# GpSimd adds the chunks for the layer norm of a projection stage, and three engines' orders change

## The chip, the cores and the metric

The kernel runs on one core of one Trainium2 chip. The metric is the device time of one execution in microseconds. Engines are named PE (TensorE), DVE (VectorE), ACT (ScalarE), POOL (GpSimd) and SP (SyncE, which here only issues DMAs).

## The reference, cut to what matters

The input `x` is (4, 1024, 256) in float32. Four blocks follow one another: latent attention, a feed-forward block, a selective scan and a second feed-forward block, each with a layer norm ahead and a residual. Only the first part of the attention is touched:

```
m = mean(x, -1); v = var(x, -1); xn = (x - m) / sqrt(v + 1e-5)
ct_q  = xn @ Wd_q_w + Wd_q_b            # 256 -> 128
query = (ct_q @ Wu_q_w + Wu_q_b) + rope(ct_q @ Wq_r_w + Wq_r_b)
ct_kv = xn @ Wd_kv_w + Wd_kv_b          # 256 -> 128
key   = (ct_kv @ Wu_k_w + Wu_k_b) + rope(xn @ Wk_r_w + Wk_r_b)
value = ct_kv @ Wu_v_w + Wu_v_b
```

## The kernel before, in words

The first stage is the function `project`. It goes over 4096 tokens in NT = 8 tiles of TW = 512 tokens. A tile is kept with its 256 features on partitions, in DC = 2 chunks `c` of 128. The stages after it (`attend`, then merging of heads, feed-forward, scan, feed-forward) are blocks of their own that begin when `project` is over.

Each engine runs a list of its own in program order, and semaphores hold an instruction until what it needs is there. An engine never passes over a waiting instruction. What a tile does:

- PE: `turn(t)` (L298) transposes tile t of x into `tr_bank`. `mean(t)` (L312) multiplies x by a matrix of 1/256, a product for each chunk, into `norm_bank`. `var(t)` (L323) does the same with the squares. `latent(t, 1)` and `latent(t, 0)` (L330) are the latent products for keys/values and for queries; `rotary` (L340), `compact` (L357) and `values` (L367) are the products behind them. A product of 128x512 in float32 takes two matmul instructions.
- ACT: `keep_x` (L427) copies the transposed tile to `xT`; `square` (L432); `guess` (L440), a first inverse root by Ln and Exp; `keep_latent` (L450); `high` (L456) and `middle` (L463) round `full` and then `rest` to bfloat16.
- DVE: `centre` (L494) subtracts the mean; `finish` (L504) does the root's Newton step in three instructions; `rotate` (L519), `join` (L533) and `keep_v` (L553) make keys, queries and values from the products.
- POOL: `scale(t)` (L266) multiplies the centred chunks by the inverse root, which gives `xn`, the input of `latent(t, 1)`. `lower_parts(t, side)` (L253) subtracts the rounded parts: first both chunks of `rest` (waiting for `high`), then both of the last part (waiting for `middle`). Side 1 is keys, side 0 queries.
- SP: the loads of x, and the stores of the three bfloat16 parts to `qk_parts`, 16 DMAs for a tile. In tile 3 it also loads the first groups' stacks.

The order on PE in a tile t is: `latent(t,1)`, `rotary(t,1)`, `latent(t,0)`, `values(t)`, `compact(t,1)`, `var(t+1)`, `rotary(t,0)`, `turn(t+2)`, `compact(t,0)`, `mean(t+2)`. ACT does `high(t-1,0)`, `keep_latent(t,1)`, `keep_latent(t,0)`, `square(t+1)`, `middle(t-1,0)`, `guess(t+1)`, `keep_x(t+2)`, `high(t,1)`, `middle(t,1)`. DVE does `rotate(t,1)`, `centre(t+1)`, `keep_v(t)`, `join(t,1)`, `finish(t+1)`, `rotate(t,0)`, `join(t,0)`. POOL does `lower_parts(t-1,0)`, `scale(t+1)`, `lower_parts(t,1)`. After the last tile PE and DVE compute row maxima for the first attention group (L413, L579).

Of the kernel before, what the change touches and what calls it, by code (L numbers as in the profile page):

```python
# [9 lines left out]
ALU = mybir.AluOpType  # L10
# [3 lines left out]
P = 128  # L14
B, S, D = 4, 1024, 256
T = B * S
TW = 512
NT = T // TW
TPB = S // TW
DC = D // P  # L20
# [108 lines left out]
def project(nc, io, xT, vT, split_scr, begun):  # L129
# [7 lines left out]
    with ExitStack() as ctx:  # L137
        m = Mem(nc, ctx)
        ident, row_max, neg_max, neg_rest, neg_parts = (
            begun[n] for n in ("ident", "row_max", "neg_max", "neg_rest", "neg_parts"))  # L140
        mean_w = m.sb("mean_w", [P, P])
# [12 lines left out]
        xc = m.sb("xc", [P, DC, TW])  # L154
        sq = m.sb("sq", [P, DC, TW])
        log_var, guess_rs, rs = (m.sb(n, [P, TW]) for n in ("log_var_p", "guess_rs_p", "rs_p"))
        xn = m.sb("xn", [P, 2, DC, TW])
        ct = m.sb("ct", [P, 2, TW])
        rot = m.sb("rot", [P, SIDES, 4, TW])
# [14 lines left out]
        proj_ready, latent_kept, rotated = m.sem("proj_ready"), m.sem("latent_kept"), m.sem("rotated")  # L174
        summed, high_kept, mid_kept = m.sem("summed"), m.sem("high_kept"), m.sem("mid_kept")
        rest_ready, low_kept, v_kept = m.sem("rest_ready"), m.sem("low_kept"), m.sem("v_kept")
        stack_in, neg_in = m.sem("first_stack_in"), m.sem("first_neg_in")
        unit_ready, unit_max, top_ready, turned, neg_ready, neg_split, ones_set = (
            m.sem(n) for n in ("unit_ready", "unit_max", "top_ready", "first_turned", "first_neg", "first_split", "first_ones"))
# [13 lines left out]
        UNITS = 12  # L193
# [6 lines left out]
        def parts_of(side):  # L200

            return (1 - side) * DC
# [41 lines left out]
        @block.gpsimd  # L244
        def _(pool):
            nc.gpsimd.memset(mean_w[:], 1.0 / D).then_inc(consts_set, 1)
            nc.gpsimd.memset(eps_col[:], EPS).then_inc(consts_set, 1)
            pool.wait_ge(consts_set, 2)
            for g in range(2):
                nc.gpsimd.memset(begun[f"ks{g}"][SROWS:MROWS], 1.0).then_inc(ones_set, 1)  # L250
                pool.wait_ge(ones_set, g + 1)

            def lower_parts(t, side):  # L253
                for u in (parts_of(side), parts_of(side) + 1):
                    k = t * CHUNKS + u
                    pool.wait_ge(high_kept, k + 1)
                    if t:

                        pool.wait_ge(low_kept, k - CHUNKS + 1)
                    nc.gpsimd.tensor_tensor(rest[:, u], full[:, u], parts[:, u, 0], ALU.subtract).then_inc(rest_ready, 1)  # L260
                for u in (parts_of(side), parts_of(side) + 1):

                    pool.wait_ge(mid_kept, t * CHUNKS + u + 1)
                    nc.gpsimd.tensor_tensor(parts[:, u, 2], rest[:, u], parts[:, u, 1], ALU.subtract).then_inc(low_kept, 1)

            def scale(t):  # L266

                pool.wait_ge(rs_step, t * 3 + 3)
                if t > 1:

                    pool.wait_ge(proj_ready, (t - 2) * UNITS + Q + 1)
                for c in range(DC):
                    nc.gpsimd.tensor_tensor(xn[:, t % 2, c], xc[:, c], rs[:], ALU.mult).then_inc(normed, 1)

            scale(0)
            for t in range(NT):
                if t:
                    lower_parts(t - 1, 0)
                if t + 1 < NT:
                    scale(t + 1)  # L280
                lower_parts(t, 1)
            lower_parts(NT - 1, 0)
            pool.wait_ge(neg_ready, 1)
            nc.gpsimd.tensor_copy(neg_parts[:, 0, 0], neg_max[:, 0]).then_inc(neg_split, 1)
            pool.wait_ge(neg_split, 1)
            nc.gpsimd.tensor_tensor(neg_rest[:, 0], neg_max[:, 0], neg_parts[:, 0, 0], ALU.subtract).then_inc(neg_split, 1)
            pool.wait_ge(neg_split, 2)
            nc.gpsimd.tensor_copy(neg_parts[:, 0, 1], neg_rest[:, 0]).then_inc(neg_split, 1)
            pool.wait_ge(neg_split, 3)
            nc.gpsimd.tensor_tensor(neg_parts[:, 0, 2], neg_rest[:, 0], neg_parts[:, 0, 1], ALU.subtract)\  # L290
                .then_inc(neg_split, 1)

        @block.tensor
        def _(pe):
# [17 lines left out]
            def mean(t):  # L312

                pe.wait_ge(x_kept, t * DC + DC)
                if t:

                    pe.wait_ge(rs_step, (t - 1) * 3 + 1)
                for c in range(DC):
                    mm = nc.tensor.matmul(norm_bank[:], mean_w[:], xT[:, c, t * TW:(t + 1) * TW],
                                          start=(c == 0), stop=(c == DC - 1))  # L320
                mm.then_inc(mean_ready, 1)

            def var(t):  # L323

                pe.wait_ge(squared, t * DC + DC)
                for c in range(DC):
                    mm = nc.tensor.matmul(norm_bank[:], mean_w[:], sq[:, c], start=(c == 0), stop=(c == DC - 1))
                mm.then_inc(var_ready, 1)

            def latent(t, u):  # L330

                if u == 0:
                    pe.wait_ge(latent_kept, t * 2 + 1)
                elif t:
                    pe.wait_ge(latent_kept, t * 2)
                for k in range(DC):
                    mm = nc.tensor.matmul(lat_bank[:], (wdq, wdkv)[u][:, k], xn[:, t % 2, k], start=(k == 0), stop=(k == DC - 1))
                mm.then_inc(proj_ready, 1)

            def rotary(t, side):  # L340
                for c in range(DC):
                    cols = slice(c * P, (c + 1) * P)
                    if side == 1:
                        if t:

                            pe.wait_ge(rotated, (t - 1) * SIDES * ROTS + ROTS + 2 * c + 2)
                        for k in range(DC):
                            mm = nc.tensor.matmul(rot_bank[c], wkr[:, k, cols], xn[:, t % 2, k],
                                                  start=(k == 0), stop=(k == DC - 1))
                    else:  # L350

                        pe.wait_ge(latent_kept, t * 2 + 2)
                        pe.wait_ge(rotated, t * SIDES * ROTS + 2 * c + 2)
                        mm = nc.tensor.matmul(rot_bank[c], wq[:, 1, cols], ct[:, 0], start=True, stop=True)
                    mm.then_inc(proj_ready, 1)
# [26 lines left out]
            mean(0)  # L382
            turn(1)
            var(0)
            mean(1)
            pe.wait_ge(consts_in, CONSTS)
            for t in range(NT):
                pe.wait_ge(normed, t * DC + DC)
                latent(t, 1)
                rotary(t, 1)  # L390
                latent(t, 0)
                values(t)
                compact(t, 1)
                if t + 1 < NT:
                    var(t + 1)
                rotary(t, 0)
                if t + 2 < NT:
                    turn(t + 2)
                compact(t, 0)
                if t + 2 < NT:  # L400
                    mean(t + 2)

            pe.wait_ge(stack_in, 2 * STACK_LOAD)
            for n in range(PAIRS):
# [18 lines left out]
        def _(act):  # L423
# [49 lines left out]
            for t in range(NT):  # L473
                if t:
                    high(t - 1, 0)
                keep_latent(t, 1)
                keep_latent(t, 0)
                if t + 1 < NT:
                    square(t + 1)
                if t:  # L480
                    middle(t - 1, 0)
                if t + 1 < NT:
                    guess(t + 1)
                if t + 2 < NT:
                    keep_x(t + 2)
                high(t, 1)
                middle(t, 1)
# [4 lines left out]
        def _(dve):  # L492
# [23 lines left out]
                nc.vector.scalar_tensor_tensor(rs[:], rs[:], 1.5, guess_rs[:], ALU.add, ALU.mult)\  # L516
                    .then_inc(rs_step, 1)

            def rotate(t, side):  # L519
                half = t % TPB  # L520
                bias = bcol[:, 2 + 4 * side:4 + 4 * side]
                cos, sin = (table[:, half * TW:(half + 1) * TW] for table in (cosT, sinT))
                r = rot[:, 1 - side]
                if t:

                    dve.wait_ge(summed, (t - 1) * CHUNKS + parts_of(side) + DC)
                for c, tables in enumerate(((cos, sin), (sin, cos))):
                    dve.wait_ge(proj_ready, t * UNITS + (ROT_K if side == 1 else ROT_Q) + c + 1)
                    for i, table in enumerate(tables):
                        nc.vector.scalar_tensor_tensor(r[:, 2 * c + i], rot_bank[c], bias[:, c:c + 1], table,  # L530
                                                       ALU.add, ALU.mult).then_inc(rotated, 1)

            def join(t, side):  # L533
                n = t * SIDES * ROTS + (1 - side) * ROTS
# [29 lines left out]
            finish(0)  # L564
            dve.wait_ge(consts_in, CONSTS)
            for t in range(NT):
                rotate(t, 1)
                if t + 1 < NT:
                    centre(t + 1)
                keep_v(t)  # L570
                join(t, 1)
                if t + 1 < NT:
                    finish(t + 1)
                rotate(t, 0)
                join(t, 0)
            for n in range(PAIRS):
                half, i = n // (PAIRS // 2), n % (PAIRS // 2)
# [1636 lines left out]
```

## Time and profile before

| | us |
|---|---|
| median of 3 runs (2103.42 to 2106.32) | 2104.65 |
| the profiled execution | 2105.05 |
| its span, first to last instruction | 2103.3 |
| PE busy | 1938.0 (92%) |
| DVE busy | 1676.9 (80%) |
| ACT busy | 1062.5 (51%) |
| POOL busy | 755.2 (36%) |
| mean granted TensorE clock | 0.955 of full speed |

Busy shares are over the whole program. `project` is its first 206 us, so these shares say little of the stage that changes; it has to be read tile by tile.

### The profile page before, as it was taken

The page shows a single profiled execution, that of the slowest core. Times are in us where ns is not written, and L with a number is a line of the kernel's source. Part 1 is how long each engine was busy: PE and PEld are TensorE (multiplying, and loading weights), DVE is VectorE, ACT ScalarE, POOL GpSimd, SP SyncE. Part 2 cuts the span into 40 slices and gives each one's busy share as a digit, 9 for nine tenths or more (in the row PEclk, how much of TensorE's full clock was granted, in tenths as well). Part 3 has the DMA queues.
Part 4 walks back from the last instruction along what each step waited for, and adds up shares of the span by engine and source line. Part 5 has one row for each costly group of instructions (what it writes and reads, how often), then busy time and mean ns, then how long its engine had stood idle before and what let it go on. Part 6 is the DMA issues. An engine that isn't in the chain of part 4 may idle for free. (4 is left out here: it accounts for less than half of the span.)

```text
span 2103.3 us, 25351 instructions
## 1 busy us (share of the span) xinstructions
PE 1938.0 (92%) x6834; PEld 728.0 (35%) x6834; DVE 1676.9 (80%) x2442; ACT 1062.5 (51%) x1399; POOL 755.2 (36%) x517
## 2 busy tenths in 40 slices
PE   8997999999999999999999997788888988799997
PEld 4441332322232323322444443233333333244443
DVE  5889998998998988964565578999999999945554
ACT  3541666665666666672222236576557557422221
POOL 4662110000000000000100029999999999810000
PEclk9996999999999999999999998999999989999998
DMA  3652112321211121213100013444444445300000
GB/s 103 142 128 52 41 42 45 66 45 42 42 47 42 41 47 41 41 50 118 40 0 0 0 62 92 125 114 118 117 115 116 117 117 152 88 0 20 20 10 31
DMA packets 94539, 138.23 MB, mean 66 GB/s; under 512 B 13600, under 2 KB 52656, under 8 KB 92880
## 3 DMA queue, kind: packets, MB, share of 16 engines
q1 hardware_dynamic: 94416, 136.73, 26.1%
q8 instruction: 61, 1.00, 0.2%
q14 instruction: 62, 0.51, 0.1%
HBM read 110.21 MB, written 26.08 MB: 65 GB/s over the span
## 5 line engine op out<-in xcount | busy, mean ns | idle before, releaser
L915 DVE TENSOR_REDUCE mx<-max_bank 128x1 f32<-128x512 f32 x960 | 617.9, 686 | 64.6 <-PE max_bank L824 64.3
L901 ACT ACTIVATE probs<-score_bank 128x1024 f32<-128x1024 f32 x512 | 496.9, 1021 | 289.2 <-PE score_bank L838 289.0
L824 PE MATMUL max_bank<-ks,qs 96*128 96x512 bf16 x960 | 335.6, 390 | 0.0
L838 PE MATMUL score_bank<-qs,ks 99*128 99x512 bf16 x1024 | 313.2, 389 | 14.9 <-issue 10.2
L1700 POOL TENSOR_TENSOR ring<-u,bc 128x1024 f32<-128x1024 f32 x128 | 302.6, 2374 | 0.0
L1770 PE MATMUL ys_bank<-outs,rec_diag 128*128 128x512 f32 x512 | 253.9, 626 | 45.6 <-POOL outs L1708 23.0
L884 PE MATMUL o_bank<-probs,vg 128*32 128x512 f32 x2048 | 275.4, 610 | 0.7 <-ACT probs L901 0.7
L1708 POOL TENSOR_TENSOR outs<-ring,bc 128x1024 f32<-128x1024 f32 x109 | 258.7, 2373 | 26.3 <-DVE ring L2079 26.3
L784 POOL CAST neg_parts<-neg_max 16x128 bf16<-16x128 f32 x31 | 8.8, 282 | 656.9 <-DVE neg_max L928 656.9
L1935 ACT ACTIVATE a_bank<-dt,decay_s 128x512 f32<-128x512 f32 x256 | 169.4, 684 | 147.4 <-DVE ring L2079 105.6
L1451 ACT ACTIVATE relu_f<-hid_bank_f 128x512 f32<-128x512 f32 x128 | 76.5, 597 | 327.3 <-PE hid_bank_f L1376 282.3
L1501 DVE SCALAR_TENSOR_TENSOR hid_f<-hid_bank_f,relu_f 128x512 f32<-128x512 f32 x128 | 86.8, 687 | 187.1 <-ACT relu_f L1451 186.1
L1352 PE MATMUL y_bank_f<-hid_f,wpr_f 128*128 128x512 f32 x512 | 234.2, 592 | 0.5 <-DVE hid_f L1501 0.5
L2070 DVE SCALAR_TENSOR_TENSOR ring<-a_bank,ring 128x512 f32<-128x512 f32 x256 | 171.4, 670 | 27.1 <-ACT a_bank L1935 26.8
L824 PEld LDWEIGHTS max_bank<-ks,qs 96*128 96x128 bf16 x960 | 94.1, 98 | 281.0 <-DVE mx L915 186.7
L1770 PEld LDWEIGHTS ys_bank<-outs,rec_diag 128*128 128x128 f32 x512 | 100.5, 200 | 186.7 <-issue 132.7
L1022 POOL TENSOR_TENSOR sq_sum_f<-sq_f 128x512 f32<-128x512 f32 x16 | 20.3, 1267 | 391.4 <-ACT sq_f L1049 391.4
L838 PEld LDWEIGHTS score_bank<-qs,ks 99*128 99x128 bf16 x1024 | 99.7, 100 | 122.9 <-issue 27.3
L1352 PEld LDWEIGHTS y_bank_f<-hid_f,wpr_f 128*128 128x128 f32 x512 | 95.9, 190 | 120.7 <-issue 115.8
L2079 DVE TENSOR_TENSOR_SCAN ring<-a_bank,ring 128x512 f32<-128x512 f32 x112 | 135.6, 1210 | 0.0
L2079 DVE TENSOR_TENSOR_SCAN ring<-a_bank,state,ring 128x512 f32<-128x512 f32 x106 | 134.7, 1271 | 0.0
L1376 PE MATMUL hid_bank_f<-xn_f,wfc_f 128*128 (+1 forms) x256 | 119.5, 600 | 3.2 <-POOL eps_col_f L991 3.2
(216 smaller groups left out, 2149.4 us busy)
## 6 DMA issues: line engine op xcount, KB each, us to landing
bc<-bc_scr SPq DMA_DIRECT2D x128, 512.0 KB, 4.9
qk_parts<-parts SPq DMA_DIRECT2D x128, 96.0 KB, 1.9
qs<-qk_parts SPq DMA_DIRECT2D x128, 64.0 KB, 4.1
o_scr<-o_sb SPq DMA_DIRECT2D x32, 256.0 KB, 2.1
ks<-qk_parts SPq DMA_DIRECT2D x16, 384.0 KB, 4.7
xin<-in_x_dram SPq DMA_DIRECT2D x8, 512.0 KB, 3.9
ks<-qk_parts SPq DMA_DIRECT2D x16, 256.0 KB, 3.5
qs<-qk_parts SPq DMA_DIRECT2D x32, 128.0 KB, 4.7
```

What stands on the lines that cost most here:

```text
L824: nc.tensor.matmul(max_bank[(r + a) % MB][:], qs[r][0:SROWS, half, j, qt * P:(qt + 1) * P], ks[r][0:SROWS, j, kh * TW:(kh + 1) * TW], star ...
L838: mm = nc.tensor.matmul(score_bank[pair][:, j % 2], ks[r][0:MROWS, j, kt * P:(kt + 1) * P], qs[r][0:MROWS, qh, j, :], start=True, stop=True)
L884: mm = nc.tensor.matmul(o_bank[32 * j:32 * j + 32, :], vg[r][:, kt, j], probs[:, s % 2, j], start=(kt == 0), stop=(kt == QT - 1))
L901: nc.scalar.activation(probs[:, s % 2, 2 * pair:2 * pair + 2], score_bank[pair][:], ACT.Exp, scale=SOFTMAX_SCALE).then_inc(probs_ready, 1)
L915: nc.vector.tensor_reduce(mx[:, a // HU, a % HU:a % HU + 1], max_bank[(r + a) % MB][:], AX_X, ALU.max)\
L1352: mm = nc.tensor.matmul(y_bank[c][:], wpr[:, f, c * P:(c + 1) * P], hid[:, f], start=(f == 0), stop=(f == FC - 1))
L1700: nc.gpsimd.tensor_tensor(ring[:, g % RING], u[t % 2][:], bc[:, g % BC, 0:1].to_broadcast([P, DC, TW]), ALU.mult).then_inc(inputs, 1)
L1708: nc.gpsimd.tensor_tensor(outs[:, g % OUTS], ring[:, g % RING], bc[:, g % BC, 1:2].to_broadcast([P, DC, TW]), ALU.mult).then_inc(weighted, 1)
L1770: mm = nc.tensor.matmul(y_bank[f][:], rec_diag[:, f * NS + n], outs[:, g % OUTS, f], start=(n == 0), stop=(n == NS - 1))
L1935: nc.scalar.activation(a_bank[g % 2][:, f], dt[:, t % 2, f], ACT.Exp, scale=a_col[:, f, n:n + 1])\
L2070: nc.vector.scalar_tensor_tensor(x, a, 1.0, x, ALU.subtract, ALU.mult).then_inc(scaled, 1)
L2079: nc.vector.tensor_tensor_scan(a if on_dve(g) else x, a, x, state[:, f, n:n + 1] if t % TPB else 0.0, ALU.mult, ALU.add)\
```

## The change

POOL adds the two chunks of x and the two chunks of the squares into new buffers `x_sum` and `sq_sum`, and for every tile but the first `mean` and `var` are then one product each in place of two. `mean(t+1)` now stands behind `latent(t,1)` in tile t (before, `mean(1)` stood ahead of the loop and `mean(t+2)` at the end of tile t). `var(t+1)` stands ahead of `compact(t,1)`. On ACT `square(t+1)` goes ahead of `keep_latent(t,0)`. On DVE `centre(t+1)` goes between the two halves of `rotate(t,1)`. On POOL `lower_parts` is cut in two functions, and the order is new.

```diff
+            def sum_x(t):
+                pool.wait_ge(x_kept, t * DC + DC)
+                if t > 1:
+                    pool.wait_ge(mean_ready, t)
+                x = slice(t * TW, (t + 1) * TW)
+                nc.gpsimd.tensor_tensor(x_sum[:], xT[:, 0, x], xT[:, 1, x], ALU.add).then_inc(x_summed, 1)
+
+            def sum_squares(t):
+                pool.wait_ge(squared, t * DC + DC)
+                if t > 1:
+                    pool.wait_ge(var_ready, t)
+                nc.gpsimd.tensor_tensor(sq_sum[:], sq[:, 0], sq[:, 1], ALU.add).then_inc(sq_summed, 1)
+
-            def lower_parts(t, side):
+            def lower_rests(t, side):
                 for u in (parts_of(side), parts_of(side) + 1):
...
                     nc.gpsimd.tensor_tensor(rest[:, u], full[:, u], parts[:, u, 0], ALU.subtract).then_inc(rest_ready, 1)
+
+            def lower_parts(t, side):
                 for u in (parts_of(side), parts_of(side) + 1):
...
             scale(0)
+            sum_x(1)
             for t in range(NT):
                 if t:
+                    lower_rests(t - 1, 0)
+                if t + 1 < NT:
+                    sum_squares(t + 1)
+                if t:
                     lower_parts(t - 1, 0)
+                lower_rests(t, 1)
                 if t + 1 < NT:
                     scale(t + 1)
+                if t + 2 < NT:
+                    sum_x(t + 2)
                 lower_parts(t, 1)
+            lower_rests(NT - 1, 0)
             lower_parts(NT - 1, 0)
```
```diff
@@ PE, mean and var
+                    pe.wait_ge(x_summed, t)
+                    nc.tensor.matmul(norm_bank[:], mean_w[:], x_sum[:], start=True, stop=True).then_inc(mean_ready, 1)
+                    return
...
+                    pe.wait_ge(sq_summed, t)
+                    nc.tensor.matmul(norm_bank[:], mean_w[:], sq_sum[:], start=True, stop=True).then_inc(var_ready, 1)
+                    return
@@ PE, order
             var(0)
-            mean(1)
             pe.wait_ge(consts_in, CONSTS)
             for t in range(NT):
                 pe.wait_ge(normed, t * DC + DC)
                 latent(t, 1)
+                if t + 1 < NT:
+                    mean(t + 1)
                 rotary(t, 1)
                 latent(t, 0)
                 values(t)
-                compact(t, 1)
                 if t + 1 < NT:
                     var(t + 1)
+                compact(t, 1)
                 rotary(t, 0)
                 if t + 2 < NT:
                     turn(t + 2)
                 compact(t, 0)
-                if t + 2 < NT:
-                    mean(t + 2)
@@ ACT, order
                 keep_latent(t, 1)
-                keep_latent(t, 0)
                 if t + 1 < NT:
                     square(t + 1)
+                keep_latent(t, 0)
@@ DVE, order (rotate now takes the chunk c)
-                rotate(t, 1)
+                rotate(t, 1, 0)
                 if t + 1 < NT:
                     centre(t + 1)
+                rotate(t, 1, 1)
                 keep_v(t)
                 join(t, 1)
                 if t + 1 < NT:
                     finish(t + 1)
-                rotate(t, 0)
+                rotate(t, 0, 0)
+                rotate(t, 0, 1)
                 join(t, 0)
```

## Rows read from the trace of the kernel before

**Rows 1.** Busy time by stretch: us, five engines (instructions), granted clock, DMA share, GB/s.
```profile
58.50:77.00 18.50, 18.33 (x53) 9.11 (x53) 15.44 (x26) 9.07 (x16) 11.49 (x11) 1.00 0.46 114
132.80:151.20 18.40, 15.69 (x40) 7.48 (x40) 15.32 (x26) 7.99 (x14) 11.39 (x11) 1.00 0.37 86
```
**Rows 2.** Waits, 20 to 165 us: total us, times, longest us.
```profile
PE lat_bank L337 <- POOL xn L273: 5.7, 8, 2.8
ACT parts L461 <- DMA qk_parts<-parts: 3.5, 2, 3.1
```
**Rows 3.** Timeline, PE in tile 1: start us, us, what, count, idle before.
```profile
39.98 1.98 PE L337 MATMUL lat_bank<-xn,wdkv 128*128 128x512 f32 x4 [0.18 <-POOL xn L273]
...
48.68 1.88 PE L363 MATMUL comp_banks<-ct,wkc 128*128 128x512 f32 x4
...
53.83 1.04 PE L308 MATMUL tr_bank<-ident,xin 128*128 128x128 f32 x8
...
54.70 1.88 PE L363 MATMUL comp_banks<-ct,wq 128*128 128x512 f32 x4
...
58.46 1.98 PE L337 MATMUL lat_bank<-xn,wdkv 128*128 128x512 f32 x4 [0.16 <-POOL xn L273]
```
**Rows 4.** Timeline, DVE, ACT and POOL in tile 1.
```profile
43.79 0.75 DVE L530 SCALAR_TENSOR_TENSOR rot<-rot_banks,bcol,cosT 128x512 f32<-128x512 f32 x1 [1.30 <-PE rot_banks L348]
...
46.76 1.27 DVE L501 TENSOR_TENSOR xc<-xT,norm_bank 128x512 f32<-128x512 f32 x2
...
51.26 1.28 DVE L550 TENSOR_TENSOR full<-comp_banks,rot 128x512 f32<-128x512 f32 x2
...
53.69 0.69 DVE L510 SCALAR_TENSOR_TENSOR rs_p<-norm_bank,guess_rs_p 128x512 f32<-128x512 f32 x1 [1.15 <-ACT guess_rs_p L448]
...
54.47 1.09 ACT L430 ACTIVATE xT<-tr_bank 128x512 f32<-128x512 f32 x2 [0.81 <-PE tr_bank L308]
...
55.44 1.15 ACT L461 ACTIVATE parts<-full 128x512 bf16<-128x512 f32 x2
...
55.91 2.50 POOL L273 TENSOR_TENSOR xn<-xc,rs_p 128x512 f32<-128x512 f32 x2 [4.16 <-DVE rs_p L516]
...
58.38 2.27 POOL L260 TENSOR_TENSOR rest<-full,parts 128x512 f32<-128x512 f32 x2
```
**Rows 5.** Timeline, end of tile 6 and tile 7.
```profile
146.61 1.88 PE L363 MATMUL comp_banks<-ct,wq 128*128 128x512 f32 x4
...
151.24 1.98 PE L337 MATMUL lat_bank<-xn,wdkv 128*128 128x512 f32 x4 [2.75 <-POOL xn L273]
...
162.53 1.28 DVE L550 TENSOR_TENSOR full<-comp_banks,rot 128x512 f32<-128x512 f32 x2
163.24 1.23 ACT L461 ACTIVATE parts<-full 128x512 bf16<-128x512 f32 x2 [3.10 <-DVE full L550]
...
163.95 2.27 POOL L260 TENSOR_TENSOR rest<-full,parts 128x512 f32<-128x512 f32 x2 [1.97 <-ACT parts L461]
```
**Rows 6.** The page's group of costliest instructions: busy us, mean ns.
```profile
L1022 POOL TENSOR_TENSOR sq_sum_f<-sq_f 128x512 f32<-128x512 f32 x16 | 20.3, 1267 | 391.4 <-ACT sq_f L1049 391.4
```
**Rows 7.** Timeline, PE behind long idle stretches in the scan.
```profile
1467.93 3.78 PE L1724 MATMUL work<-xT,mean_w_s 128*128 128x512 f32 x4 [5.52 <-DVE dt L2039]
1471.50 3.12 PE L1770 MATMUL ys_bank<-outs,rec_diag 128*128 128x512 f32 x4
...
1541.82 3.39 PE L1724 MATMUL work<-xT,mean_w_s 128*128 128x512 f32 x4 [4.80 <-DVE dt L2039]
...
1614.36 3.45 PE L1724 MATMUL work<-xT,mean_w_s 128*128 128x512 f32 x4 [5.79 <-DVE dt L2039]
...
1761.07 3.48 PE L1724 MATMUL work<-xT,mean_w_s 128*128 128x512 f32 x4 [4.66 <-DVE dt L2039]
```
**Rows 8.** Busy time by stretch, columns as in Rows 1, behind one of them.
```profile
1761.00:1764.40 3.40, 3.33 (x5) 1.51 (x6) 3.40 (x5) 1.94 (x4) 3.40 (x2) 0.54 1.01 210
```
**Rows 9.** Timeline, PE ahead of tile 0.
```profile
13.18 1.98 PE L327 MATMUL norm_bank<-sq,mean_w 128*128 128x512 f32 x4 [0.33 <-ACT sq L438]
...
21.51 1.96 PE L337 MATMUL lat_bank<-xn,wdkv 128*128 128x512 f32 x4 [1.95 <-POOL xn L273]
```

More of the change, by code:

```diff
@@ L156, in project @@
         log_var, guess_rs, rs = (m.sb(n, [P, TW]) for n in ("log_var_p", "guess_rs_p", "rs_p"))
+        x_sum, sq_sum = m.sb("x_sum", [P, TW]), m.sb("sq_sum", [P, TW])
         xn = m.sb("xn", [P, 2, DC, TW])
@@ L176, in project @@
         rest_ready, low_kept, v_kept = m.sem("rest_ready"), m.sem("low_kept"), m.sem("v_kept")
+        x_summed, sq_summed = m.sem("x_summed"), m.sem("sq_summed")
         stack_in, neg_in = m.sem("first_stack_in"), m.sem("first_neg_in")
@@ L325, in var @@
                 pe.wait_ge(squared, t * DC + DC)
+                if t:
+                    pe.wait_ge(sq_summed, t)
+                    nc.tensor.matmul(norm_bank[:], mean_w[:], sq_sum[:], start=True, stop=True).then_inc(var_ready, 1)
+                    return
                 for c in range(DC):
@@ L517, in finish, with rotate @@
                     .then_inc(rs_step, 1)
-            def rotate(t, side):
+            def rotate(t, side, c):
                 half = t % TPB
@@ L526, in rotate @@
                     dve.wait_ge(summed, (t - 1) * CHUNKS + parts_of(side) + DC)
[L527 to L531, printed above, removed]
+                dve.wait_ge(proj_ready, t * UNITS + (ROT_K if side == 1 else ROT_Q) + c + 1)
+                for i, table in enumerate(((cos, sin), (sin, cos))[c]):
+                    nc.vector.scalar_tensor_tensor(r[:, 2 * c + i], rot_bank[c], bias[:, c:c + 1], table,
+                                                   ALU.add, ALU.mult).then_inc(rotated, 1)
             def join(t, side):
```

## The prediction

> **What bounds the kernel now.** The page's busy shares are averages over six stages, and only the first stage changes. So I read four views: busy time by stretch with one stretch per tile, the waits of the stage, the timeline of one whole tile, and the timeline of places where PE idled long.
>
> In a middle tile PE is busy 18.33 of 18.50 us [rows 1]. That looks like a stage bound by PE. The tile from 132.8 us says otherwise: it has no transposition and no product for a mean, PE does 15.69 us of work in it, and the tile still takes 151.24 - 132.77 = 18.47 us, with a wait of 2.75 us at its end for `xn` from POOL [rows 1, 2, 5]. The reader is to see that two bounds lie on top of one another: PE's work, and a loop of dependences that runs from `latent(t,1)` over the products ahead of `var(t+1)`, then guess, Newton step and scaling, to `latent(t+1,1)`. Even the other tiles end in a wait for `xn`, of 0.18 us [rows 3]. Taking work off PE gains only if that loop gets shorter too. So the sum has to follow the loop in the new orders. I count from T = 0, the start of `latent(t,1)`.
>
> **PE's work.** The transposition in tile 1 starts at 53.83 - 39.98 = 13.85 [rows 3], behind 16 products of about 0.86 us. In the new order there are 16 as well: two for the latent, one for the mean, four for `rotary`, two each for `latent(t,0)` and `values`, one for the variance, two each for `compact` and `rotary(t,0)`. The transposition stays at 13.85, and `compact(t,0)` starts at 14.72 and ends at 16.60 [rows 3]. Nothing comes behind it now. What falls away is the pair for the mean behind it, 1.72 us in a tile.
>
> **The two sums on POOL.** An addition of this shape took 1.27 us [rows 6]. The sum of x follows `scale`, ends about 1.2, and `mean` is at 1.8: hidden. For the squares: the first rotation began at 43.79 - 39.98 = 3.81 [rows 4], now one product later, 4.67. Two rotations of 0.67 take DVE to 6.0. The centring pair (1.27) ends at 7.3; the second square, 0.6 us like the copies of x [rows 4], ends at 7.95; the sum on POOL ends at 9.3. PE comes to `var` at 9.55. It is hidden with 0.25 us to spare; if the cover went, every 0.1 us over it would cost 0.1 in each of 7 tiles. `square` ahead of `keep_latent(t,0)` and `centre` between the rotations cost nothing: the latter makes the second half of `rotate` end at 8.7, where DVE waits for `values` anyway. I put all of it at 0, with -0.1 to +0.3 a tile as bounds.
>
> **The Newton step moves behind a later `join`.** `compact(t,1)` started at 48.68 - 39.98 = 8.70 [rows 3] and now has two products more ahead of it: 10.42. The last pair of `join` starts 51.26 - 48.68 = 2.58 later [rows 3, 4], at 13.00, and ends at 14.28. `finish` is behind it on DVE and then takes 55.91 - 53.69 = 2.22 until POOL can scale [rows 4]: 16.50. Before, `scale` began at 55.91 - 39.98 = 15.93. So although `var` is ready sooner, the inverse root comes 0.57 us later: what was a wait for the guess (1.15 us, [rows 4]) is now a wait for `compact`.
>
> **The scaling now stands behind `lower_rests(t,1)` on POOL.** This is the dear part. The two `rest` subtractions wait for `high(t,1)` on ACT. ACT's order is unchanged there: `keep_x(t+2)` stands ahead of `high(t,1)`, and it waits for the transposition at 13.85. The trace has `keep_x` at 54.47 and `high` at 55.44 = T + 15.46 [rows 4]. POOL starts 163.95 - 163.24 = 0.71 after `high` does [rows 5]: 16.17. Two subtractions of 2.27 (less a few ns of overlap) end at 18.42, 1.92 after the inverse root was there. Before, they stood behind the scaling and cost nothing [rows 4]. From the start of `scale` to `latent` it is 58.46 - 55.91 = 2.55 [rows 3, 4], so `latent(t+1,1)` starts at 20.97. Before it was 58.46 - 39.98 = 18.48. That is +2.49 in each of six tiles (0 to 5, those with a transposition): **+14.9 us**.
>
> Tile 6 has no transposition. There `high` follows `join` by 163.24 - 162.53 = 0.71 [rows 5]: 13.71, POOL 14.42, the subtractions end at 16.67, `latent(7,1)` starts at 19.22 in place of 18.47: **+0.75 us**.
>
> `high` also waited up to 3.1 us for its stores once [rows 2], in tile 4, since the stack loads stood ahead of them in SP's queue. That would now delay the scaling. The stores' place hangs on earlier tiles, which grow by more than 3 us together, so I put it at 0, at most 3 us once.
>
> **The clock.** With PE done at 16.60 and the next start at 20.97, PE idles 4.4 us in each of six tiles; 19.22 - 15.72 = 3.5 us ahead of tile 7; and ahead of tile 0 from 15.16 to 21.51 = 6.35 us [rows 9], since `mean(1)` no longer lies there. The trace has seven idle stretches of 4.66 to 7.64 us in the scan, each right behind dense matmuls. Behind all seven the first matmuls took about double: 3.39 to 3.78 us for four in place of 1.98 [rows 7], at a granted clock of 0.54 in a stretch shown [rows 8], so mostly the lower level, 1.2 GHz. The time lost was 1.5 us (at 1614.36 and 1761.07) to 3.0 us (at 1467.93, with the group behind it at 3.12 in place of 1.88), and 2.0 in the mean of the seven. Against it: behind the idle 2.75 us at 151.24 nothing was lost [rows 5]. 4.4 is nearest to 4.66, so I take 2.0 for the six and for tile 0, and 1.2 for tile 7, whose 3.5 lies between the two. From `latent` to the transposition PE is the path, so all of it counts: 8 starts, 2.0 x 7 + 1.2 = **+15.2 us**. Bounds: 0, and 8 x 3.0 = 24.
>
> The Trainium skill (TensorE: Matmul & The Clock Gate, HAM oscillation — how this bites in real kernels) says the same of a loop whose every tile makes PE wait: the clock is lowered in the wait and the cost is paid anew in every tile, where a loop that keeps PE fed pays once. The trace agrees for the long stretches, by the doubled durations. By that rule the term is due; if the scan's rows did not carry over, the sum would end at 15.7 and not 30.9.
>
> **Sum.** 14.9 + 0.75 + 15.2 = 30.9 us. The profiled execution took 2105.05 (its span 2103.3 and 1.75 around it), which gives 2135.9; the median of the runs is 0.4 below that execution, so 2135.5. The stages behind are unchanged, and they begin when this one ends.
>
> **Rivals.**
> (a) The same wait, but the clock holds over 4.4 us of idle. For it: the 2.75 us row. Against: seven of seven from 4.66 on. 2104.65 + 15.7 = 2120.3, up to 2123 if tile 0 alone is hit.
> (b) The subtractions don't hold `scale`, since `high(t,1)` comes sooner than I read; then the late `join` alone sets it: 0.57 x 7 = 4.0, and idle of about 2.5 a tile costs the clock little, at most some 6 us. 2108.6 to 2115. Against it: ACT's order is written out, and the transposition's place on PE doesn't move.
> (c) Faster. PE is the bound, and the loop isn't: with 1.72 us less work in each of 7 tiles the time falls by 12.0 to 2092.6. It decides if `scale` can begin at 14.1 or sooner, so that `xn` is there when PE ends at 16.60. For it: 18.33 of 18.50 busy. Against: the tile from 132.8, and `join`, `finish` and the subtractions, which stand in front of it by program order.
> (d) Slower still: the sum of squares misses its 0.25 us, the stores' wait shows, and the clock costs 3.0 each time: 2145.
>
> **How the numbers follow.** Forecast 0.66, (a) 0.14, (b) 0.08, (c) 0.06, (d) 0.06. The forecast's own range is 2128 to 2142 (clock 1.0 to 2.8 for each start). To hold 8 in 10, the range takes in (a) below: 2117 to 2142. About 0.2%, 4.2 us, is what a measurement can tell from no change. Slower by more: the forecast, (a), (d) and most of (b), 0.92; faster: 0.05 of (c); within: 0.03.
>
> **What would show it.** In the changed trace: `rest` (L260's line) ahead of `xn` on POOL with a wait for `parts` of ACT of some 4 us; `latent` to `latent` 21 us plus what the clock takes, 23 in all; a PE wait for `xn` of 4.4 us in six tiles; the first matmuls of tiles at double duration; `finish` directly behind `join`, with no wait for the guess; no wait of `var` for `sq_sum`. It is wrong if `scale` starts before T + 18 in the middle tiles, or if tiles take less than 18.5.

## The result, and the profile after

| | before | after |
|---|---|---|
| median, us | 2105.21 (2103.42 to 2106.32, 4 runs) | 2135.32 (2133.57 to 2136.17, 4 runs) |
| profiled execution, us | 2105.05 | 2136.12 |
| its span | 2103.3 | 2134.3 |
| POOL busy | 755.2 | 773.2 |
| ratio | | 1.0142, 95% interval 1.013 to 1.0155 |

Four executions of the kernel before in the later sets took 2151 to 9001 us; they are slow ones and stand in no median here.

The change makes the kernel 30.1 us slower; 30.9 was forecast. Two tiles of PE's timeline in the changed kernel, to be laid beside [rows 3]:

```profile
44.60 3.78 PE L373 MATMUL lat_bank<-xn,wdkv 128*128 128x512 f32 x4 [4.37 <-POOL xn L292]
48.17 1.85 PE L347 MATMUL norm_bank<-x_sum,mean_w 128*128 128x512 f32 x2
49.87 3.60 PE L384 MATMUL rot_banks<-xn,wkr 128*128 128x512 f32 x8
...
56.74 1.02 PE L360 MATMUL norm_bank<-sq_sum,mean_w 128*128 128x512 f32 x2
57.60 1.88 PE L399 MATMUL comp_banks<-ct,wkc 128*128 128x512 f32 x4
...
61.03 1.04 PE L336 MATMUL tr_bank<-ident,xin 128*128 128x128 f32 x8
61.91 1.88 PE L399 MATMUL comp_banks<-ct,wq 128*128 128x512 f32 x4
68.15 3.78 PE L373 MATMUL lat_bank<-xn,wdkv 128*128 128x512 f32 x4 [4.36 <-POOL xn L292]
```

A tile takes 68.15 - 44.60 = 23.55 us where it took 18.48. PE waits 4.36 us for `xn` (4.4 was forecast), and then four matmuls take 3.78 in place of 1.98. Busy time by stretch shows the clock, for a whole tile and for the start of it:

```profile
68.15:91.87 23.72, 19.36 (x49) 9.39 (x49) 15.27 (x26) 9.57 (x17) 13.98 (x13) 0.86 0.36 89
68.10:71.70 3.60, 3.55 (x4) 1.51 (x5) 0.56 (x1) 1.23 (x2) 3.60 (x4) 0.50 0.10 22
```

The start runs at 0.50 of full speed, 1.2 GHz. DVE, ACT and POOL around the end of the tile that starts at 44.60, answering to [rows 4]:

```profile
55.20 1.28 POOL L268 TENSOR_TENSOR sq_sum<-sq 128x512 f32<-128x512 f32 x1 [4.98 <-ACT sq L473]
...
60.19 1.28 DVE L584 TENSOR_TENSOR full<-comp_banks,rot 128x512 f32<-128x512 f32 x2
61.38 0.68 DVE L545 SCALAR_TENSOR_TENSOR rs_p<-norm_bank,guess_rs_p 128x512 f32<-128x512 f32 x1
61.67 1.09 ACT L465 ACTIVATE xT<-tr_bank 128x512 f32<-128x512 f32 x2 [2.52 <-PE tr_bank L336]
62.64 1.15 ACT L496 ACTIVATE parts<-full 128x512 bf16<-128x512 f32 x2
62.82 0.69 DVE L551 SCALAR_TENSOR_TENSOR rs_p<-rs_p,guess_rs_p 128x512 f32<-128x512 f32 x1
63.35 2.29 POOL L277 TENSOR_TENSOR rest<-full,parts 128x512 f32<-128x512 f32 x2 [4.58 <-ACT parts L496]
...
65.61 2.49 POOL L292 TENSOR_TENSOR xn<-xc,rs_p 128x512 f32<-128x512 f32 x2
```

The Newton step ends at 63.51, and the scaling begins at 65.61, directly behind the subtractions. These waited 4.58 us for `high` (L496), which stands behind `keep_x` (L465), which waited for the transposition. The squares' sum ends at 56.48, 0.26 before `var` starts at 56.74 with no wait.

### The profile page after: what moved, and what is told of

Same layout as the page of the kernel before. It is cut to its first block and busy times, and to the rows that moved or that the text cites. A ratio compares the mean times of both kernels' runs of the same rounds, so it can differ in the third digit from the quotient of the medians.

```text
span 2134.3 us, 25342 instructions
## 1 busy us (share of the span) xinstructions
PE 1938.3 (91%) x6806; PEld 728.7 (34%) x6806; DVE 1678.0 (79%) x2442; ACT 1065.7 (50%) x1399; POOL 773.2 (36%) x531
```

## The experiments

All times are medians beside runs of the kernel before on the same chip (2106.3, 2105.2 and 2106.3 us in the three sets). Differences are of these medians as they stand; where two kernels come from different sets they carry about 1 us of the sets' own difference. What a change is worth in the stage is read from the profiled execution of each kernel.

**The scaling first.** The changed kernel with:

```diff
-                lower_rests(t, 1)
                 if t + 1 < NT:
                     scale(t + 1)
                 if t + 2 < NT:
                     sum_x(t + 2)
+                lower_rests(t, 1)
                 lower_parts(t, 1)
```

> The changed kernel with one edit on POOL: the scaling (and the sum of x) stands ahead of lower_rests(t,1) again. Theory (the scaling is held by the subtractions that wait for high(t,1)): scale starts at T + 16.5 when the Newton step ends, latent to latent is 19.05 us, PE idles 2.4 us a tile; with the clock kept up there, 0.57 x 7 = 4.0 us over the kernel before, and 2 us for the cold start of tile 0: 2111, up to 2118 if 2.4 us of idle still lowers the clock in some tiles. Rival (PE's new order with the mean behind the latent is what costs): no change, 2135.

Measured: 2116.61 us, ratio 1.0047 (1.0029 to 1.0065). The POOL edit alone takes back 18.7 of the 30 us. PE's timeline:

```profile
43.17 2.59 PE L373 MATMUL lat_bank<-xn,wdkv 128*128 128x512 f32 x4 [2.35 <-POOL xn L292]
58.72 1.04 PE L336 MATMUL tr_bank<-ident,xin 128*128 128x128 f32 x8
63.83 2.76 PE L373 MATMUL lat_bank<-xn,wdkv 128*128 128x512 f32 x4 [2.35 <-POOL xn L292]
```

From the transposition to the next latent it is 5.11 us; it was 7.12. The tile is 20.66 and not 19.05 long, since from the latent to the transposition it takes 15.55 and not 13.85: behind only 2.35 us of idle the clock still costs 1.7 us, in each of the six tiles that have it. The theory holds for the wait, and its upper value (2118) for the clock.

**`high` first.** The changed kernel with:

```diff
+                high(t, 1)
                 if t + 2 < NT:
                     keep_x(t + 2)
-                high(t, 1)
                 middle(t, 1)
```

> The changed kernel with one edit on ACT: high(t,1) stands ahead of keep_x(t+2), POOL's order is left as changed. Theory (it is the wait for the transposition, passed on through ACT's queue, that makes the subtractions late): high starts at T + 13.7, the subtractions end at 16.67, latent to latent is 19.2 us, and the time is 0.75 x 7 + 2 over the kernel before: 2112, up to 2119 with clock losses. Rival (the two subtractions in front of the scaling cost their own 2.3 us wherever they stand): 7 x 2.3 = 16 over it, 2121 and more.

Measured: 2129.81 us, ratio 1.0109 (1.0091 to 1.0127). Only 5.5 us come back. The theory's 2112 to 2119 is missed, and the time lies in the rival's range, but the rival's mechanism (2.3 us a tile) isn't what the trace has: from the transposition to the next latent it is 6.47 us, against 5.11 with the scaling first and 5.35 by the theory. ACT does what was meant: `high` now starts 0.13 us ahead of the transposition (59.67 and 59.80), so at T + 13.72 at full clock. But then:

```profile
59.67 1.23 ACT L496 ACTIVATE parts<-full 128x512 bf16<-128x512 f32 x2 [1.75 <-DVE full L584]
...
60.15 0.68 DVE L545 SCALAR_TENSOR_TENSOR rs_p<-norm_bank,guess_rs_p 128x512 f32<-128x512 f32 x1
60.38 2.72 POOL L277 TENSOR_TENSOR rest<-full,parts 128x512 f32<-128x512 f32 x2 [2.83 <-ACT parts L496]
...
60.87 1.22 DVE L548 SCALAR_TENSOR_TENSOR rs_p<-rs_p,guess_rs_p 128x512 f32<-128x512 f32 x1
...
62.12 1.52 DVE L551 SCALAR_TENSOR_TENSOR rs_p<-rs_p,guess_rs_p 128x512 f32<-128x512 f32 x1
...
63.72 2.49 POOL L292 TENSOR_TENSOR xn<-xc,rs_p 128x512 f32<-128x512 f32 x2 [0.62 <-DVE rs_p L551]
```

The subtractions now run beside the second and third instruction of the Newton step. These take 1.22 and 1.52 us in place of 0.69, and POOL's pair 2.72 in place of 2.27. The scaling waits for the Newton step again, later than before. In one tile the wait for the stores adds to it (PE waits 6.65 us there and 3.7 ahead of five others). Behind four of these five the clock was low as before; behind the fifth nothing was lost:

```profile
110.89 1.98 PE L373 MATMUL lat_bank<-xn,wdkv 128*128 128x512 f32 x4 [3.72 <-POOL xn L292]
```

**One more addition beside the Newton step.** To show that by itself, the kernel with the scaling first got in `scale(t)`, from tile 1 on:

```diff
+                    pool.wait_ge(rs_step, t * 3 + 1)
+                    nc.gpsimd.tensor_tensor(unused[:], xT[:, 0, 0:TW], xT[:, 1, 0:TW], ALU.add).then_inc(beside, 1)
                 pool.wait_ge(rs_step, t * 3 + 3)
```

> The kernel with the scaling ahead of lower_rests(t,1), and on POOL one more addition of two 128x512 tiles (into an unused buffer), let go by the first of the Newton step's three instructions, so that it runs beside the second and third. In the kernel with high(t,1) first these two took 1.22 and 1.52 us beside POOL's subtractions and 0.69 each in the other kernels. Theory (the two engines slow one another where the DVE instruction reads two operands from SBUF): they stretch again to 1.2 and more, scale starts 0.8 to 1.4 us later: 7 x 1.1 = 8 us over 2116.6, 2124. Rival (it was something else, and the addition of 1.27 us fits into POOL's idle time): 2116.6.

Measured: 2125.45 us, ratio 1.0098 (1.0078 to 1.0118). Groups by line, first this kernel, then the one without the addition:

```profile
L557 DVE SCALAR_TENSOR_TENSOR rs_p<-rs_p,guess_rs_p 128x512 f32<-128x512 f32 x7 | 11.5, 1643 | 0.2
L292 POOL TENSOR_TENSOR unused<-xT 128x512 f32<-128x512 f32 x7 | 12.0, 1707 | 26.3 <-DVE rs_p L551 26.3
```
```profile
L551 DVE SCALAR_TENSOR_TENSOR rs_p<-rs_p,guess_rs_p 128x512 f32<-128x512 f32 x7 | 4.8, 692 | 0.2
L261 POOL TENSOR_TENSOR x_sum<-xT 128x512 f32<-128x512 f32 x7 | 8.9, 1270 | 0.0
```

The third instruction went from 0.69 to 1.64 us and the addition from 1.27 to 1.71. The second (0.69, not shown) had begun before the addition and was not slowed. So the slowing is shown: 0.95 us a tile, 6.7 in all, and in the profiled executions the first maxima begin 7.0 us later (191.17 against 184.13). Where the rest of the 8.8 us between the medians lies was not found. PE's waits grew to 3.30 us; behind five of the six in tiles 1 to 6 the clock was low, behind the first (at 42.48) it was not.

**The clock kept up.** The changed kernel with filler:

```diff
+            def fill(n):
+                for _ in range(n):
+                    nc.tensor.matmul(lat_bank[:], mean_w[:], xT[:, 0, 0:TW], start=True, stop=True)
             for t in range(NT):
+                fill(7 if t == 0 else 5 if t < NT - 1 else 4)
                 pe.wait_ge(normed, t * DC + DC)
```

> The changed kernel with filler products on PE: 7 products of the mean's matrix with x into lat_bank ahead of tile 0, 5 ahead of tiles 1 to 6, 4 ahead of tile 7 (0.86 us each, 4.3 of the 4.37 us that PE waits). Their results are overwritten; nothing else changes. Theory (the clock falls in the wait and makes the first matmuls slow, 2.0 us and more a tile): all tiles run at 2.4 GHz, latent to latent is 21.0 us, and the time falls to 2105.2 + 14.9 + 0.75 = 2121. Rival (slow first matmuls cost nothing since the chain behind them waits anyway): 2135 or more.

Measured: 2117.58 us, ratio 1.0048 (1.003 to 1.0066).

```profile
42.20 1.98 PE L373 MATMUL lat_bank<-xn,wdkv 128*128 128x512 f32 x4
56.05 1.04 PE L336 MATMUL tr_bank<-ident,xin 128*128 128x128 f32 x8
...
63.19 1.99 PE L373 MATMUL lat_bank<-xn,wdkv 128*128 128x512 f32 x4
```

More matmuls, less time: 17.7 us of the change's 30 are gone with the clock kept up. The tile is 20.99 us, split as forecast: 13.85 to the transposition, 7.14 from there (forecast 7.12). One tile has 22.45, with the wait for the stores. The whole is 3.4 us below the 2121 expected, and not because the stage was shorter: the first maxima begin 17.7 us later than before (184.24 against 166.59), where 15.65 were expected. Attention is 3.5 us shorter (744.2 and 747.7), of which more below.

**Both edits: the scaling first, the clock kept up.** `fill(7 if t == 0 else 2 if t < NT - 1 else 3)` in the kernel with the scaling first.

> The kernel with the scaling ahead of lower_rests(t,1), and filler products into lat_bank on PE: 7 ahead of tile 0, 2 ahead of tiles 1 to 6, 3 ahead of tile 7. It leaves only the late join. Theory: all tiles at 2.4 GHz, from the transposition to the next latent 5.1 us as without the filler, latent to latent 18.96 us, 0.48 x 7 = 3.4 us over the kernel before: 2109. Rival (the clock takes nothing at 2.35 us of idle): 2116.6 as without the filler.

Measured: 2103.81 us, ratio 0.9991 (0.9981 to 1.0001): not to be told from the kernel before.

```profile
40.17 1.98 PE L373 MATMUL lat_bank<-xn,wdkv 128*128 128x512 f32 x4 [0.64 <-POOL xn L292]
...
59.13 1.98 PE L373 MATMUL lat_bank<-xn,wdkv 128*128 128x512 f32 x4 [0.63 <-POOL xn L292]
```

The tile is 18.96 us, as expected, but the whole is 5 us less than expected. The stage ends 2.8 us late (211.2 against 208.4 for the first scores) where 3.4 were expected; the rest of the 5 us lies in the attention stage (743.3 us in place of 747.7), below.

**The squares' sum alone.** The kernel before with `sum_squares` on POOL and `var` as one product, all other orders kept. On POOL:

```diff
                 if t:
-                    lower_parts(t - 1, 0)
+                    lower_rests(t - 1, 0)
+                if t + 1 < NT:
+                    sum_squares(t + 1)
+                if t:
+                    lower_parts(t - 1, 0)
                 if t + 1 < NT:
                     scale(t + 1)
+                lower_rests(t, 1)
                 lower_parts(t, 1)
```

> The kernel before with only the squares' sum moved to POOL: one product for var from tile 1 on, lower_parts cut in two with the sum between its halves, the scaling ahead of lower_rests(t,1); all orders of PE, ACT and DVE and both products of the mean are as before. Theory (a loop of dependences over var, guess, Newton step and scaling bounds the tile together with PE): the sum on POOL ends at about T + 10.2, under the products of compact, so 0.86 us less work ahead of the guess and on PE: latent to latent 17.6 us, 7 x 0.86 = 6 us faster, 2099. Rival (POOL's sum is late, or DVE's join holds the Newton step): 2105 or slower.

Measured: 2104.2 us, ratio 0.999 (0.998 to 1.0001). Six tiles are 17.68 us long, as expected, and one is 23.45:

```profile
112.58 0.63 ACT L483 ACTIVATE parts<-full 128x512 bf16<-128x512 f32 x1 [5.80 <-DMA qk_parts<-parts]
...
118.98 2.57 PE L359 MATMUL lat_bank<-xn,wdq 128*128 128x512 f32 x4 [3.86 <-ACT ct L475]
```

`high` waits 5.80 us for its stores, `keep_latent` is queued behind it on ACT, and PE waits for that; then the clock is low. So the time is where the rival put it (2105), but neither of the rival's causes is in the trace: what ate the gain was a wait that no expectation had.

**The stack loads spread.** The same kernel; SP issues its 26 stack loads in four lots ahead of the stores of tiles 3 to 6:

```diff
-                    for g in range(2):
-                        load_stack(sp, split_scr, begun[f"qs{g}"], begun[f"ks{g}"], g, stack_in)
+                if TPB + 1 <= t < TPB + 5:
+                    for dst, src in stacks[(t - TPB - 1) * 7:(t - TPB) * 7]:
+                        sp.dma_start(dst, src).then_inc(stack_in, 16)
```

> The kernel with only the squares' sum on POOL, and SP's 26 loads of the first groups' stacks no longer all in tile 3 but 7, 7, 7 and 5 of them in tiles 3 to 6. The trace of the squares-only kernel has six tiles of 17.7 us and one of 23.45, in which high waited 5.8 us for its stores to qk_parts. Theory (the stack loads ahead of the stores in SP's queue cause that): the tile comes down to 17.7, and the time to 2104.2 - 5.8 = 2098.5. Rival (SP's queue is full anyway with 16 stores in 12 us of a 17.7 us tile): the wait only moves to other tiles, 2102 to 2106.

Measured: 2099.77 us, ratio 0.9972 (0.996 to 0.9983). All seven tiles take 17.65 to 17.70 us from latent to latent. The tile that was long now starts at 109.94:

```profile
109.94 1.98 PE L369 MATMUL lat_bank<-xn,wdkv 128*128 128x512 f32 x4 [0.17 <-POOL xn L294]
127.62 1.98 PE L369 MATMUL lat_bank<-xn,wdkv 128*128 128x512 f32 x4 [0.18 <-POOL xn L294]
```

The stack loads ahead of the stores in SP's queue were what held them.

**A new order with both sums.** The parts that helped, with the chain shortened as the traces showed:

```diff
@@ PE
                 latent(t, 1)
-                if t + 1 < NT:
-                    mean(t + 1)
-                rotary(t, 1)
+                rotary(t, 1, 0)
+                if 0 < t < NT - 1:
+                    mean(t + 1)
+                rotary(t, 1, 1)
                 latent(t, 0)
-                values(t)
+                compact(t, 1)
                 if t + 1 < NT:
                     var(t + 1)
-                compact(t, 1)
+                values(t)
...
-                if t + 2 < NT:
-                    turn(t + 2)
                 compact(t, 0)
+                if t + 2 < NT:
+                    turn(t + 2)
@@ DVE
-                keep_v(t)
                 join(t, 1)
                 if t + 1 < NT:
                     finish(t + 1)
+                keep_v(t)
@@ POOL
                 if t + 1 < NT:
                     scale(t + 1)
+                lower_rests(t, 1)
                 if t + 2 < NT:
                     sum_x(t + 2)
                 lower_parts(t, 1)
```

On ACT `high(t, 1)` is ahead of `keep_x(t + 2)` and `keep_latent(t, 1)` ahead of `high(t - 1, 0)`; `mean(1)` is back ahead of the loop.

> A new order with both sums on POOL. PE: latent(t,1), first half of rotary, mean(t+1), second half, latent(t,0), compact(t,1), var(t+1), values, rotary(t,0), compact(t,0), turn(t+2); mean(1) with two products ahead of the loop as in the kernel before. DVE: join and finish ahead of keep_v. ACT: keep_latent(t,1) ahead of high(t-1,0), high(t,1) ahead of keep_x(t+2). POOL: scale, lower_rests(t,1), sum_x, lower_parts(t,1). Stack loads spread. Theory: compact is early, so join ends at T + 11.8 and the Newton step follows the guess at 12.05; scale starts at 14.2 and latent to latent is 16.8 to 17.2 us with PE and DVE both nearly full: 7 x 1.5 = 10.5 us faster, 2095 (2092 to 2099). Rival (POOL and SP, at 14 and 12 us in each tile, are now in the way): 2100 and more.

Measured: 2088.32 us, ratio 0.992 (0.990 to 0.9939). Run again:

> The new order with both sums on POOL once more, for the interval: 2088, 0.992 of the kernel before (0.990 to 0.994), with 16.87 us from latent to latent in six tiles.

Measured: 2087.99 us, ratio 0.9911 (0.9894 to 0.9929). It beats both kernels, by 18 and 47 us.

```profile
37.49 1.98 PE L383 MATMUL lat_bank<-xn,wdkv 128*128 128x512 f32 x4 [0.17 <-POOL xn L302]
...
48.00 1.28 DVE L597 TENSOR_TENSOR full<-comp_banks,rot 128x512 f32<-128x512 f32 x2
...
49.57 0.69 DVE L558 SCALAR_TENSOR_TENSOR rs_p<-norm_bank,guess_rs_p 128x512 f32<-128x512 f32 x1 [0.29 <-ACT guess_rs_p L496]
...
51.79 2.51 POOL L302 TENSOR_TENSOR xn<-xc,rs_p 128x512 f32<-128x512 f32 x2 [2.61 <-DVE rs_p L564]
...
54.36 1.98 PE L383 MATMUL lat_bank<-xn,wdkv 128*128 128x512 f32 x4 [0.17 <-POOL xn L302]
```

A tile is 16.87 us long (the first 15.9). `join` ends before the guess is there, so the Newton step waits for the guess alone; the scaling starts at T + 14.3; POOL is idle beside the Newton step; and PE's wait is 0.17 us, and behind it no latent is slow. The tile is as long as expected (16.8 to 17.2), but the time is under the expected 2092 to 2099. The first maxima begin 13.0 us earlier than before (153.62 against 166.59), 2.5 more than the 10.5 counted, and attention is 4.2 us shorter (743.5), which was not counted. In the second run of this kernel the profiled execution began tile 0 at the low clock (3.75 us for the first four matmuls) where the first run's did not (1.96); the tiles behind are as long in both.

**Names only.** The kernel before with `x_sum`, `sq_sum` and their semaphores declared and unused.

> The kernel before with the change's two buffers and two semaphores declared and never used; no instruction of the projection differs. It asks why the attention stage, whose code nobody changed, took 748 us from its first to its last scores in the kernels with up to one new semaphore and 741 to 744 in those with two. Theory (layout or numbering of semaphores shifts it): attention 743, the whole 2100.5. Rival (it hangs on how the projection ran, or on chance): attention 748, the whole 2105.4.

Measured: 2105.0 us, ratio 0.9994 (0.9983 to 1.0005); attention took 957.9 - 212.1 = 745.8 us. The whole is the rival's (2105.4), and the theory's 2100.5 lies outside the interval (2102.7 to 2107.4), so the names are not what shortens the program; the one profiled attention lies between the two. The same trace shows what chance does. PE's instructions and their order are those of the kernel before, and so is the wait ahead of tile 7:

```profile
151.80 3.78 PE L339 MATMUL lat_bank<-xn,wdkv 128*128 128x512 f32 x4 [2.75 <-POOL xn L275]
```

Here the clock was low behind 2.75 us of idle, and the way to the first maxima took 18.36 us in place of 15.35; in the trace of the kernel before the same 2.75 us cost nothing [rows 5].

## Why the prediction was right, step by step

**The bound: right.** The loop of dependences bound the tile, not PE: with two products less in a tile and neither the held scaling nor the clock against it (18.96 us) it was still longer than before (18.48), and PE waited some 0.64 us for `xn` in each. The squares' sum alone can't tell the two bounds apart, since it took one product out of PE's work and out of the loop as well: 0.82 us (18.50 to 17.68).

**The two sums: right.** `var` never waited; 0.26 us were left and 0.25 forecast.

**The Newton step behind a later `join`: right.** With the scaling first and the clock up, the tile is 18.96 us; 16.50 + 2.55 = 19.05 was the sum.

**The scaling behind the subtractions: right.** 7.12 us from the transposition to the next latent in all six tiles, exactly the forecast (20.97 - 13.85). Putting the scaling back took 2.0 of it away.

**Tile 6: the mechanism right, the size short.** From `compact(t,0)` to the latent it took 6.47 us; forecast was 19.22 - 13.84 = 5.38. Without a transposition `high` comes early, and the subtractions fall beside the Newton step (timeline of the changed kernel):

```profile
180.74 2.72 POOL L277 TENSOR_TENSOR rest<-full,parts 128x512 f32<-128x512 f32 x2 [2.84 <-ACT parts L496]
181.23 1.22 DVE L548 SCALAR_TENSOR_TENSOR rs_p<-rs_p,guess_rs_p 128x512 f32<-128x512 f32 x1
...
182.48 1.52 DVE L551 SCALAR_TENSOR_TENSOR rs_p<-rs_p,guess_rs_p 128x512 f32<-128x512 f32 x1
```

So the term was 1.8 and not 0.75.

**The stores' wait: right at 0.** The same 7.12 us stand in tile 4. It hung on the slow tiles: with 21.0 us tiles 1.5 us of it showed, with `high` first 2.9, and with 17.7 us tiles 5.8.

**The clock: right that it falls, mis-sized.** The term was 2.0 for tile 0 and for tiles 1 to 6, and 1.2 for tile 7, 15.2 together. Latent to transposition (to the last `compact` in tiles 6 and 7), less what it takes at full clock, gives 2.22 in tile 0, 2.58 to 2.93 in tiles 1 to 6, 1.55 in tile 7: 20.7. The mean of [rows 7] was too low for it: in most tiles the low clock outlasts the first four matmuls and reaches the mean's product (1.9 in place of 1.02) and `rotary` (up to 3.92 in place of 3.60), as in the dearest row of before, the one at 1467.93. Rival (b) rested on 2.5 us of idle costing little, since the 2.75 us row cost nothing. That was wrong: behind 2.35 us it cost 1.7 in each of tiles 1 to 6. The 1.2 us for tile 7 came from the same row, and that row was chance: with names only, the same wait cost 3.0. One row without a loss is no threshold.

**The sum: right in part by luck.** The stage's terms add up to 14.9 + 1.8 + 20.7 = 37.4, and the first maxima begin 203.52 - 166.59 = 36.9 us later (timeline of PE, before and after; tile 0 began 0.1 earlier, and a tile of before had 0.3 of its own, which no longer shows):

```profile
166.59 0.59 PE L413 MATMUL rot_banks<-ks,qs 96*128 96x512 bf16 x2 [1.33 <-DVE rot L530]
```
```profile
203.52 0.59 PE L448 MATMUL rot_banks<-ks,qs 96*128 96x512 bf16 x2 [1.33 <-DVE rot L564]
```

The whole is 31.0 later. The prediction took the stages behind as unchanged, which holds for their code and not for their time: 5.9 us came back in stages whose code is the same, mostly in attention, whose first and last scores are, before and after:

```profile
L838 PE MATMUL score_bank<-qs,ks x1024: 377/379/634, 208.4 to 956.1; 99*128 99x512 bf16 x171
```
```profile
L874 PE MATMUL score_bank<-qs,ks x1024: 377/379/634, 245.3 to 988.4; 99*128 99x512 bf16 x171
```

That is 747.7 and 743.1 us. It is 747.9 and 748.4 in the two kernels with the squares' sum alone, 745.8 with names only, and 739.7 to 744.2 in the others. Chance is part of it: 743.5 and 739.7 are one kernel, the new order, executed twice. The stage's loop stops PE for 2.4 to 3.1 us four times, and the clock's answer differs. In the 12 us behind the four stops the granted clock was 0.74, 0.58, 0.72 and 0.72 before, and 1.00, 0.86, 0.74 and 0.74 after; in the shortest attention (739.7) it was 1.00, 0.86, 1.00 and 0.86, in the longest (748.4) 0.72 each time. Busy time by stretch around the first stop, before and after:

```profile
352.00:360.00 8.00, 8.00 (x28) 2.61 (x27) 5.09 (x8) 4.20 (x5) 0.00 (x0) 0.64 0.01 3
```
```profile
389.00:397.00 8.00, 8.00 (x43) 2.50 (x41) 7.12 (x12) 5.71 (x6) 0.00 (x0) 1.00 0.01 3
```

So the shorter attention goes with a clock that falls less behind these stops. Why it falls less in every trace that has both sums than in those without stays open. Rivals (a) and (b) fall with the doubled matmuls and the 7.12 us, (c) with the longer tile, (d) with the 0.26 us left over; of its parts only the larger clock cost came, and only in part (2.6 a start in the mean, where it had 3.0). So the forecast of 30.9 met 30.1 because terms some 6.5 us too small (5.5 of the clock, 1.05 in tile 6) stood against 5.9 us that came back where nothing was changed.

## What to carry to other kernels

Before an instruction is put ahead of another on an in-order engine, follow what it waits for through every queue: here two subtractions waited for a copy behind a copy behind a transposition, and the tile's critical scaling inherited all of it. Where PE's busy share and a loop over the other engines are both near the tile's length, taking work off PE opens idle time, and idle time is paid a second time in the clock; shorten the loop first. Price such idle from several rows, and by how long the matmuls behind stay slow, not only the first group; and take a wait that once cost nothing as a matter of chance until a second trace says the same.

## What the runs showed of the hardware that was not expected

POOL's additions of two SBUF tiles and DVE instructions that read two SBUF tiles slow one another: 0.69 to 1.64 us on DVE, 1.27 to 1.71 on POOL. DVE instructions with one operand in PSUM (`rotate`) kept 0.74 us beside POOL's scaling, and the scaling its 1.27. The Trainium skill (GPSIMD Engine Reference, Key points) says that the two engines share their interfaces to SBUF and contend where a VectorE instruction has two SBUF inputs; the trace agrees, by these numbers.

The length of one idle stretch did not decide here whether the clock fell. Idle stretches of 2.35 us on PE lost it in six tiles of six (the scaling first) and 4.36 us in six of six (the changed kernel), but 3.30 us in five of six (one more addition) and 3.7 us in four of five (`high` first). At one and the same place, ahead of tile 7, 2.75 us lost nothing in the kernel before [rows 5] and with the stack loads spread, and lost it with names only (3.78 us for the four matmuls) and, at 2.76, in the squares-only kernel (3.68).
